# SiLU of a gated feed-forward written with tanh: one activation replaced by two on ScalarE and one more product on VectorE

## The reference, cut to what matters

```python
xn = _layernorm(x, axis=-1)
x = x + _L0_attn_ref(xn, ...) + _L0_ffn_ref(xn, ...)     # gelu, hidden width 2048
xn = _layernorm(x, axis=-1)
x = x + _L1_attn_ref(xn, ...) + _L1_ffn_ref(xn, ...)     # rotary, causal; gated
```

```python
x12 = jnp.einsum('bsk,mk->bsm', x, w12) + b12
x1, x2 = jnp.split(x12, 2, axis=-1)      # 512 + 512 wide
x4 = jax.nn.silu(x1) * x2
return jnp.einsum('bsm,nm->bsn', x4, w3) + b3
```

## Time and profile before

| | |
|---|---|
| time, median of 3 runs | 619.87 us (619.39 to 623.91) |
| the profiled execution | 624.43 us, span 622.3 us |
| TensorE busy (PE) | 577.9 us, 93% of the span |
| VectorE busy (DVE) | 451.5 us, 73% |
| ScalarE busy (ACT) | 356.0 us, 57% |
| GpSimd busy (POOL) | 217.8 us, 35% |
| mean granted TensorE clock | 0.981 of full speed |

### The profile page before, as it was taken

The page is one execution under the profiler, slowest core; times in us unless marked ns, Lnnn a source line. Parts: engine busy times, 40 slices in busy tenths (PEclk is TensorE's granted clock), DMA queues, the critical chain, the costliest instruction groups (busy, mean ns, idle before and its releaser), DMA issues.

```text
span 622.3 us, 10485 instructions
## 1 busy us (share of the span) xinstructions
PE 577.9 (93%) x3232; PEld 443.3 (71%) x3232; DVE 451.5 (73%) x1198; ACT 356.0 (57%) x611; POOL 217.8 (35%) x332
## 2 busy tenths in 40 slices
PE   2698899999999999999999998899989989899997
PEld 2686677787777878667777777677767877666754
DVE  6559967656566675576897677889997988578663
ACT  3337766755555683676694575657655654465541
POOL 5712423122303321211223122354644555254241
PEclk9999899999999999999999999989999999988989
DMA  5583542353223244315443332425433344334101
GB/s 186 176 241 127 141 115 67 105 153 103 68 86 103 70 131 124 86 45 160 120 136 101 95 90 74 120 85 139 141 98 102 86 127 130 87 102 116 23 5 63
DMA packets 29806, 67.29 MB, mean 108 GB/s; under 512 B 4788, under 2 KB 17588, under 8 KB 27704
## 3 DMA queue, kind: packets, MB, share of 16 engines
q1 hardware_dynamic: 21112, 38.32, 22.2%
q0 software_dynamic: 8640, 28.32, 15.6%
HBM read 51.67 MB, written 14.68 MB: 107 GB/s over the span
## 4 chain that ended last, share of the span: by engine, by line
PE 73%; DVE 9%; ACT 6%; issue 5%; DMA 5%; POOL 1%; SPq 1%; ACTq 0%; DVEq 0%; POOLq 0%
PE banks L692 49%; PE banks L745 8%; PE banks L771 7%; PE banks L793 7%; DMA q_sb<-q_parts 2%; DVE banks L1065 1%; DMA q_sb<-max_t 1%; ACT L910 1%; PE banks L774 1%; PE banks L712 1%; ACT hid_f L930 1%; ACT L929 1%; DVE bn L976 1%; ACT probs L910 1%; DVE x_res L1109 1%
## 5 line engine op out<-in xcount | busy, mean ns | idle before, releaser
L910 ACT ACTIVATE probs<-banks 128x512 f32<-128x512 f32 (+1 forms) x256 | 137.6, 545 | 185.1 <-PE banks L771 143.9
L692 PE MATMUL banks<-xnT,w_up 128*128 128x512 f32 x576 | 154.7, 403 | 5.4 <-issue 3.8
L1070 DVE TENSOR_REDUCE neg_max<-banks 128x2 f32<-128x512 f32 x128 | 87.1, 687 | 93.2 <-PE banks L745 92.6
L692 PE MATMUL banks<-w_down,hid 128*128 128x512 f32 x480 | 131.1, 407 | 4.5 <-ACT hid_f L930 2.0
L692 PEld LDWEIGHTS banks<-xnT,w_up 128*128 128x128 f32 x576 | 103.4, 192 | 33.9 <-issue 15.1
L1065 DVE CUSTOM_DVE_ANT_0 banks<-banks,mask_qk 128x128 f32<-128x128 f32 (+1 forms) x256 | 86.3, 374 | 39.4 <-PE banks L745 39.4
L692 PEld LDWEIGHTS banks<-w_down,hid 128*128 128x128 f32 x480 | 87.7, 193 | 32.3 <-DVE neg_max L1070 6.7
L745 PEld LDWEIGHTS banks<-k_sb,q_sb 96*128 96x128 f32 x512 | 93.7, 193 | 23.3 <-issue 5.2
L745 PE MATMUL banks<-k_sb,q_sb 96*128 96x256 f32 (+1 forms) x512 | 100.8, 279 | 5.2 <-DMA q_sb<-q_parts 4.0
L648 POOL TENSOR_SCALAR_AFFINE_SELECT probs<-probs 128x256 f32<-128x256 f32 x128 | 59.6, 466 | 102.6 <-ACT probs L910 97.5
L771 PE MATMUL banks<-q_sb,k_sb 97*128 97x512 f32 x192 | 79.9, 416 | 8.8 <-ACT probs L910 6.9
(11 more groups left out here) (77 smaller groups left out, 651.3 us busy)
## 6 DMA issues: line engine op xcount, KB each, us to landing
q_sb<-q_parts SPq DMA_DIRECT2D x64, 256.0 KB, 4.4
raw<-in_up POOLq DMA_DIRECT2D x48, 256.0 KB, 3.0
raw<-in_down POOLq DMA_DIRECT2D x40, 256.0 KB, 3.1
q_parts<-stage SPq DMA_DIRECT2D x32, 256.0 KB, 2.5
raw<-in_attn POOLq DMA_DIRECT2D x20, 256.0 KB, 3.2
k_parts<-stage SPq DMA_DIRECT2D x16, 256.0 KB, 2.6
k_sb<-k_parts SPq DMA_DIRECT2D x16, 256.0 KB, 4.0
x_res<-in_x SPq DMA_DIRECT2D x4, 512.0 KB, 4.0
```

The costliest lines, as they stand in the source:

```text
L692: mm = nc.tensor.matmul(out_ap, lhs(a), rhs(b_), start=first and j == 0, stop=stop and j == 2, **kw)
L910: nc.scalar.activation(probs[:, i, 0:w], banks[:, ST_BANKS[k % 2], 0:w], ACT.Exp, scale=SCALES[n // B]).then_inc(exp_done, 1)
L1070: nc.vector.tensor_reduce(neg_max[:, s, 2 * g:2 * g + 2, t], banks[:, bank_of[x], :].rearrange("p (r t) -> p r t", r=2)[:, :, 0:w], AX.X, ...
```

## The change

SiLU(z) with z = x + b is written as (z/2) x (1 + tanh(z/2)).

- `gate`: instead of one SiLU, ScalarE now does two activations that read the same bank: Tanh of 0.5 x + b/2 into `hid_f[:, 0]`, and Identity of 0.5 x + b/2 into a new tile `gate_f`. The semaphore `gate_done` is raised by the second.
- `hidden`: VectorE first computes (`hid_f[:, 0]` + 1) x `gate_f` into `gate_f`, both operands in SBUF, waits for itself on the new semaphore `gate_full`, and then does the product of before with `gate_f`.
- once, at the step `bias` in the start-up: VectorE halves the four bias columns of the gate into `bias_half`; the first `gate` waits for it.

```diff
@@ scalar @@
-                    cc = 16 + c % CHUNKS[1]
-                    nc.scalar.activation(hid_f[:, 0, :], banks[:, bank_of["up", 1, c, 0], :], ACT.Silu,
-                                         bias=bias_up[:, cc:cc + 1]).then_inc(gate_done, 1)
+                    if c == 0:
+                        act.wait_ge(half_made, 1)
+                    bank = banks[:, bank_of["up", 1, c, 0], :]
+                    half = bias_half[:, c % CHUNKS[1]:c % CHUNKS[1] + 1]
+                    nc.scalar.activation(hid_f[:, 0, :], bank, ACT.Tanh, bias=half, scale=0.5)
+                    nc.scalar.activation(gate_f[:, :], bank, ACT.Identity, bias=half, scale=0.5).then_inc(gate_done, 1)
@@ vector @@
+                if x[0] == "bias":
+                    dve.wait_ge(c_loaded, 48)
+                    nc.vector.tensor_scalar(bias_half[:, :], bias_up[:, 16:16 + CHUNKS[1]], 0.5, None, ALU.mult).then_inc(half_made, 1)
@@ vector, hidden of layer 1 @@
+                    nc.vector.scalar_tensor_tensor(out=gate_f[:, :], in0=hid_f[:, 0, :], scalar=1.0, in1=gate_f[:, :],
+                                                   op0=ALU.add, op1=ALU.mult).then_inc(gate_full, 1)
+                    dve.wait_ge(gate_full, c + 1)
                     cc = 20 + c % CHUNKS[1]
                     nc.vector.scalar_tensor_tensor(out=hid_f[:, 1, :], in0=banks[:, bank_of["up", 1, c, 1], :],
-                                                   scalar=bias_up[:, cc:cc + 1], in1=hid_f[:, 0, :],
+                                                   scalar=bias_up[:, cc:cc + 1], in1=gate_f[:, :],
                                                    op0=ALU.add, op1=ALU.mult).then_inc(full_done, 1)
```

More of the change, by code:

```diff
@@ L367, in build @@
         hid_f = sb("hid_f", [P, 2, 512])
+        gate_f = sb("gate_f", [P, 512])
         xn = sb("xn", [P, TT, D])
@@ L388, in build @@
         bias_up = sb("bias_up", [P, 24])
+        bias_half = sb("bias_half", [P, CHUNKS[1]])
         bias_out = sb("bias_out", [P, 2, D], F32R)
@@ L437, in build @@
         up_done = sem("up_done")
+        half_made = sem("half_made")
         gate_done = sem("gate_done")
+        gate_full = sem("gate_full")
         full_done = sem("full_done")
```

## The result

The changed kernel takes 625.52 us in the median of 20 runs (622.23 to 631.2); the kernel before, run beside it, 623.16 us (20 runs; the 619.87 above is the median of its first three). The ratio is taken between the means, without the one run of the kernel before that was far slower than its others (631.21 us): 1.0061 with a 95% interval of 1.0035 to 1.0086, slower by 3.8 us (2.2 to 5.4). The medians alone are 2.4 us apart. Forecast were +3.1 us and no change beyond 1%.

A forecast was written before the change was run, and what follows sets the result against it. TensorE, busy for 93% of the span, was taken to bound the kernel. Product cost 4.4 us less gain 1.3 us gave +3.1 us on a 619.87 us median: 622.9 us, range 616.5 to 627.5 us.

The forecast's parts named there:

- The product's cost: VectorE's added product at the hidden steps: 6 x 0.73 = 4.4 us lost, bounds 2.2 and 6.0.
- the six places: Hidden steps c = 0, 1, 2, 3, 4 and 6, each forecast to cost the product's full 0.73 us.
- The two places taken for free: Hidden steps c = 5 (VectorE idle afterwards) and c = 7 (next scores wait for an exponential): product charged 0.
- The gain: TensorE's waits returned at the gates without table loads: 0.87 + 0.32 + 0 + 0.11 = 1.3 us, bounds 0 and 2.4.
- all of that returns: Gate c = 1: the scores' whole 0.87 us wait for the exponential comes back, the exponential being 2.1 us earlier.
- Gate 2: Behind gate c = 2, at most 2.24 - 1.92 = 0.32 us can return before the maxima's DMA decides.
- Gate 4: Behind gate c = 4 TensorE waits 1.31 us for the maxima's DMA anyway, so its 0.42 us is worth nothing.
- The 1.92 us from issue to matmul: Time from issue of the row maxima's DMA to the waiting matmul, used as the limit behind gates 2 and 6.
- 2.1 us are freed at each: At each gate the exponential starts about 1.2 us after the first load's former start instead of 3.3 us.
- The loads on the chain: Rival at gates 1, 2 and 6: 2.1 us each, 6.3 us back against 4.4, so -1.9 us, 618.0 us; chance 0.20.
- The clock: Rival: lengthened TensorE waits bring two more half-clock stretches, +6.5 us, 626.4 us; chance 0.18.
- Nothing to see: Rival: slack in VectorE's queues meets the product and gains are uncovered waits, about 620.3 us; chance 0.12.

The follow-up runs named there:

- The product alone: Kernel before with SiLU and its table loads kept, plus VectorE's added product and wait at all eight hidden steps, result unused; ratio 1.0085 to the kernel before.
- The loads alone: Kernel before with Tanh in place of SiLU at the gate, so 16 table loads go, without Identity or product; ratio 0.9976 to the kernel before.
- double-product runs: Changed kernel with one more product of the same kind behind the first at each hidden step; ratio 1.0117 to the kernel before.
- swap alone: Kernel before with the load of the queries for unit u + 2 issued ahead of the load of the keys; ratio 0.9964 to the kernel before.

## Why the prediction was right

The direction, the size (+3.1 us forecast, +3.8 measured, interval 2.2 to 5.4) and the mechanism hold: what ScalarE saves TensorE hardly waits for, and what VectorE adds stands in front of the row maxima. The absolute forecast, 622.9 us, fell 2.6 us short of the 625.52 because it was carried onto a median of three runs, 619.87, that lies 3.3 us under the median of twenty; that it stayed inside the range owes something to the range's width. And the two terms of the sum were not equally good.

*The product's cost, 4.4 us forecast.* The product alone measures +5.3 us (3.1 to 7.5), at equal clock 3.9 (1.2). By TensorE's steps in that run the six places give 0.70 (c = 0), 0.26 (1), 0.38 (2), 0.71 (3), 0.35 (4) and 0.93 (6), together 3.3, against 6 x 0.73 = 4.4; c = 5 gives 0 and c = 7 gives +0.73 and -0.73. Another 0.35 us stands just ahead of c = 1, where the queries took 7.82 us to land instead of 7.47, and is not the product's. The two places taken for free were free, and each of the six others cost something in this run, but at c = 2 and 4 only half is paid and at c = 1 a third: 0.73 us was right for three places of six, and too much for the others. The rest up to the run's 3.9 us at equal clock is inside its 1.2. The places c = 0 and c = 6 in the changed kernel, to be set against the earlier trace rows:

```profile
398.90 0.93 DVE L1129 SCALAR_TENSOR_TENSOR gate_f<-hid_f,gate_f 128x512 f32<-128x512 f32 x1
399.88 0.75 DVE L1133 SCALAR_TENSOR_TENSOR hid_f<-banks,bias_up,gate_f 128x512 f32<-128x512 f32 x1
400.66 0.62 ACT L955 CAST hid<-hid_f 128x512 fp32r<-128x512 f32 x1 [1.84 <-DVE hid_f L1133]
400.68 0.44 PE L749 MATMUL banks<-k_sb,q_sb 96*128 96x128 f32 x2 [0.69 <-DVE hid_f L1133]
...
405.64 0.69 PE L775 MATMUL banks<-q_sb,k_sb 97*128 97x512 f32 x1 [2.70 <-ACT probs L914]
```
```profile
571.87 0.75 DVE L1133 SCALAR_TENSOR_TENSOR hid_f<-banks,bias_up,gate_f 128x512 f32<-128x512 f32 x1
...
573.30 0.52 SPq L575 DMA_DIRECT2D q_sb<-max_t  x1
...
575.39 0.47 PE L775 MATMUL banks<-q_sb,k_sb 97*128 97x512 f32 x1 [1.20 <-DMA q_sb<-max_t]
```

ScalarE's wait for the hidden product went from 0.87 to 1.84 us, and the wait for the maxima from 0.37 to 1.20 us (+0.83). At c = 0 I had missed a second path: line 749 now waits 0.69 us for the hidden step directly, a wait that was not there before. The 2.70 us behind it stayed as they were, since ScalarE and TensorE are both later by the same amount.

*The gain, 1.3 us forecast.* The loads alone measure -1.5 us (-3.0 to 0), at equal clock 0.0 (0.8), so the size is not refuted, but it was put together wrongly, and that the net forecast still fits is partly luck: both terms were too large, which cancels in their difference. The step "all of that returns", 0.87 us at gate 1, failed: I checked the exponential and the maxima there, but not the next wait in the queue, the queries of unit 20, which had 0.09 us of slack. Gate 2 gave what was said, next to nothing: -0.78 us and then +0.7 back at the first scores. At gate 6 -0.80 us are followed by +1.25, but a stretch of half clock lies there and not at the same matmuls in both traces, so its net is not read. Gate 4, given as nothing, kept 0.76 us in the loads-alone run and 0.98 in the changed kernel. The 1.92 us from issue to matmul, which priced gates 2 and 6, is not one figure either: at gate 4, where TensorE waits for the same DMA, it is 505.19 - 502.60 = 2.59 us. And "2.1 us are freed at each" was too much: at gate 1 Tanh itself waits 0.72 us for its operand,

```profile
421.14 0.69 ACT L947 ACTIVATE hid_f<-banks,bias_half 128x512 f32<-128x512 f32 x1 [0.72 <-PE banks L696]
421.72 0.68 ACT L948 ACTIVATE gate_f<-banks,bias_half 128x512 f32<-128x512 f32 x1
422.29 1.08 ACT L914 ACTIVATE probs<-banks 128x512 f32<-128x512 f32 x2
```

and against TensorE's clock of work (1.97 us late at this point) the exponential comes 421.78 + 1.97 - 422.29 = 1.5 us earlier. The Trainium skill, ScalarE: Activation LUTs, section What ACT_TABLE_LOAD costs, would have a switch cost 2.66 us with its drain, so by an estimate from it two of them 5.3 us, less the added activation; the trace shows nothing of that drain: before, SiLU starts 1.29 us after the start of its load (418.49 to 419.78), and the exponential 1.29 us after the start of the next (420.49 to 421.78).

*The rivals.* The loads on the chain: refuted by the loads alone. The clock: a mean of 0.9851 (0.0016 either way) in the changed kernel's runs and 0.9851 in those of before, so no price of the clock is seen there, to within 0.8 us; in the product-alone (0.9818) and double-product runs (0.9813) the mean is lower, and there the clock may be a part of the price, which nine and six runs do not settle. Nothing to see: refuted by the interval. The start-up instruction, charged nothing, was not run apart; the product alone, which comes without it, already costs as much as the whole change.

## What to carry to other kernels

A table load in front of an activation can lie in the wait for its operand, so count what the engine behind it waits for, not the loads. When a wait goes, go on along the queue to the next transfer and ask for its slack; one that lands 0.1 us ahead of its use takes the gain. Work that is added to an engine with a quarter of its time free is still paid when it stands right ahead of what opens the next unit: here 3.3 to 3.9 us for 5.8 us of work, against 1.2 us where that engine waits soon after. And before a step between two traces is put down to a change, check that it does not stand at a transfer whose time varies by itself.

## What the runs showed that I had not expected

The granted clock drops to 0.50 for stretches of 3.4 or 6.8 us at places that differ from run to run of one kernel, and this goes with most of the scatter between runs: 2.4 us without and 1.4 us with the clock taken out, at 0.52 us for each 0.001. It let the slower kernel show the shorter profile. With the swap alone the mean clock is 0.9877 (0.0015 either way) against 0.9851, so at its own clock the kernel gains more (ratio 0.9964, -2.2 us) than at equal clock (-1.2 us); whether its shorter waits bring the better clock is not shown. And the order of two DMA issues of 0.5 to 1 us moved the landing of the queries in unit 28 by 2.5 us (542.01 to 539.56): 1.15 us because they were issued earlier (536.54 to 535.39), and 1.3 us because they took less time from issue to landing, 4.16 us instead of 5.47. At unit 20 the second part is 3.4 us (7.47 to 4.08).
